# Deformable convolution in a four-layer kernel: GpSimd issues the second chunk's loads, hats go in three lots, and constant products run in a wait

## What is computed

```python
x = x + _L3_conv_ref(_gn(x), L3_conv_weight, L3_conv_bias, L3_conv_off_w, L3_conv_off_b, L3_conv_mask_w, L3_conv_mask_b)

offset = conv2d(x, off_w, off_b)                 # dy, dx for each of 9 taps, image and pixel
mask = jax.nn.sigmoid(conv2d(x, mask_w, mask_b))
samp = deform_sample(x, offset, mask)            # bilinear samples of x at moved places, times mask
out = jnp.einsum('bckhw,ock->bohw', samp, weight.reshape(O, C, K * K))
return out + bias[None, :, None, None]
```

## Time and profile before

| | us |
|---|---|
| median of 3 runs | 539.01 (535.24 to 540.68) |
| the profiled execution | 540.11 |
| its span | 538.3 |

### The profile page before, as it was taken

One profiled execution on the slowest core, in us unless ns is written; L12 is line 12 of the kernel. 1 busy time (PEld: TensorE's weight loads), 2 busy tenths in 40 slices (PEclk: granted clock), 3 DMA queues, 4 the chain that ended last, 5 costly groups with the idle time before them and its releaser, 6 DMA issues. The chain is left out here.

```text
span 538.3 us, 9045 instructions
## 1 busy us (share of the span) xinstructions
PE 421.3 (78%) x3242; PEld 211.8 (39%) x3242; DVE 342.4 (64%) x668; ACT 295.2 (55%) x515; POOL 132.9 (25%) x162
## 2 busy tenths in 40 slices
PE   1415672399999863858999999965977999999995
PEld 1213551245554432512333333333533545455442
DVE  4437787403334537897999999434365878788784
ACT  1359993105145413705888888852675668486441
POOL 4420002200000000665442211104063618155000
PEclk9855997579999956865999999995999999999999
DMA  5500000530000000493220000006464290743302
GB/s 139 160 0 1 0 0 0 119 76 0 1 1 0 1 0 0 127 311 113 82 80 2 4 2 2 2 1 148 99 188 101 58 208 2 185 80 64 70 2 78
DMA packets 20765, 33.77 MB, mean 63 GB/s; under 512 B 5656, under 2 KB 15496, under 8 KB 19956
## 3 DMA queue, kind: packets, MB, share of 16 engines
q1 hardware_dynamic: 16724, 23.70, 18.2%
q0 software_dynamic: 2176, 6.35, 4.3%
q10 hardware_dynamic: 1824, 3.19, 2.2%
HBM read 16.21 MB, written 4.64 MB: 39 GB/s over the span
## 5 line engine op out<-in xcount | busy, mean ns | idle before, releaser
L1308 DVE TENSOR_TENSOR L_s<-L_row_ps,L_cols 128x1024 f32<-128x1024 f32 x72 | 87.7, 1219 | 7.1 <-PE L_row_ps L1473 6.5
L884 DVE TENSOR_REDUCE L_mx<-L_ring 128x2 f32<-128x512 f32 x128 | 83.3, 687 | 10.9 <-PE L_ring L1007 10.3
L939 ACT ACTIVATE L_e<-L_ring 128x512 f32<-128x512 f32 x128 | 73.8, 598 | 20.8 <-PE L_ring L1020 18.8
L1496 PE MATMUL L_acc<-L_s,L_t_sb 128*64 128x256 f32 x576 | 78.0, 392 | 1.4 <-DVE L_s L1308 1.2
L1377 ACT ACTIVATE L_cols<-L_col_ps 128x512 f32<-128x512 f32 x72 | 42.9, 597 | 47.4 <-PE L_col_ps L1483 47.0
L1007 PE MATMUL L_ring<-stacks_k_st,stacks_q_st 64*128 64x256 bf16 x256 | 50.8, 301 | 6.3 <-DVE L_v_all L873 4.6
L1496 PEld LDWEIGHTS L_acc<-L_s,L_t_sb 128*64 128x64 f32 x576 | 34.9, 136 | 34.3 <-DVE L_s L1308 20.7
L1020 PE MATMUL L_ring<-stacks_q_st,stacks_k_st 64*128 64x256 bf16 x256 | 47.1, 281 | 1.3 <-DMA stacks_q_st<-L_m_parts 1.3
L1473 PE MATMUL L_row_ps<-L_hats,L_sel 48*128 48x512 bf16 x144 | 43.2, 381 | 0.0
L1040 PE MATMUL L_ctx_ps<-L_e,L_v_x 128*32 128x256 f32 x512 | 41.1, 395 | 0.0
L370 PE MATMUL L_y<-L_t,all_w_post 128*128 128x256 f32 x96 | 25.1, 416 | 14.3 <-DVE L_t L330 14.3
(11 more groups left out here) (267 smaller groups left out, 788.0 us busy)
## 6 DMA issues: line engine op xcount, KB each, us to landing
L_hats<-L_parts SPq DMA_DIRECT2D x28, 216.0 KB, 4.9
L_hat<-L_offsets SPq DMA_DIRECT2D x20, 192.0 KB, 4.7
L_mask<-L_offsets SPq DMA_DIRECT2D x10, 192.0 KB, 5.1
stacks_q_st<-L_q_parts SPq DMA_DIRECT2D x12, 128.0 KB, 3.9
stacks_k_st<-L_k_parts ACTq DMA_DIRECT2D x12, 128.0 KB, 4.8
stacks_q_st<-L_q_parts POOLq DMA_DIRECT2D x12, 128.0 KB, 2.7
stacks_k_st<-L_k_parts POOLq DMA_DIRECT2D x12, 128.0 KB, 2.9
L_stack<-L_xpad SPq DMA_DIRECT2D x7, 162.0 KB, 5.9
```

Of the source, the lines that this page charges most:

```text
L884: dve.tensor_reduce(mx[:, n % 2, :, head], ring[:, place(step) % 3].rearrange("p (q s) -> p q s", q=2), AX.X, ALU.max).then_inc(max_read, 1)
L939: act.activation(e[:, k], ring[:, 3 + v % 3], ACT.Exp, scale=HD2 ** -0.5).then_inc(e_ready, 1)
L1308: dve.tensor_tensor(s[:, q], row_ps[:, q], cols[:, t % 3:t % 3 + 1].broadcast_to([P, 2, 2 * N]), ALU.mult).then_inc(s_ready, 1)
L1496: mm = pe.matmul(acc[C * e:C * e + C, b, 0:N], t_sb[:, b, h, (KK * e + t) * C:(KK * e + t + 1) * C], s[:, q, h, e * N:(e + 1) * N], start= ...
```

## The change

- **Constant products.** A new function `keep_clock` multiplies the constant `avg2` by itself into a part of `row_ps` that nobody reads: five times after the GroupNorm, then two, two and four times behind the first three `weigh` products.
- **Weigh products.** Three instead of four stand ahead of the first convolution; the fourth comes behind it, and the fifth between `spread_positions(1)` and `spread_masks(1)`.
- **VectorE and ScalarE at the start.** VectorE's copies of the first three products come between the `xpad` steps; ScalarE loads the sigmoid table behind `take_t` of the third product rather than ahead of all.
- **Hats of pair 0 in three lots** of one third each, the second with a semaphore of its own (`second_third_in`, awaited at v = 3).
- **Loads of chunk 1** are issued by GpSimd, between its stores of quad 1 and those of quads 2 and 3. Positions and masks now share one semaphore; for chunk 1 the first third has one (awaited at 48), the second and the last third share another (awaited at 96).
- **`hat_steps`**: the distance and the hat of the last third come ahead of `take_first` of the first third.

The core of the diff:

```diff
+def keep_clock(pe, avg2, out, count):
+    for _ in range(count):
+        pe.matmul(out[:, 0:P], avg2[:], avg2[:], start=True, stop=True)
...
-        hat_in, mask_in = m.sems("hat_in0 hat_in1 hat_in2"), m.sems("mask_in0 mask_in1 mask_in2")
+        hat_in, second_chunk_in, second_third_in = m.sems("hat_in0 hat_in1 hat_in2"), m.sems("second_chunk_in0 second_chunk_in1"), m.sem("second_third_in")
+        def chunk_in(c, j):
+            if c == 1:
+                return (second_chunk_in[0], 48) if j == 0 else (second_chunk_in[1], 96)
+            return hat_in[j], 48 * (c - 1) + (48 if j == 2 and c else 96 if j == 2 else 0)
...
                 sp.wait_ge(off_stored, 128)
-                load_positions(sp, 0, 2)
-                load_masks(sp, 0, 2)
+                load_chunk(sp, 0, 2)
+                sp.wait_ge(parts_ready, 1)
+                send_hats(0, slice(0, THIRD))
                 sp.wait_ge(parts_ready, 2)
-                send_hats(0, slice(0, 2 * THIRD))
-                sp.wait_ge(later_stored, 128)
-                sp.wait_ge(hat_in[2], 32)
-                sp.wait_ge(mask_in[2], 16)
-                for j in range(3):
-                    load_positions(sp, 1, j)
-                    load_masks(sp, 1, j)
+                send_hats(0, slice(THIRD, 2 * THIRD), second_third_in)
                 sp.wait_ge(parts_ready, 3)
...
                 store_masks(pool, slice(1, 2), later_stored)
+                pool.wait_ge(later_stored, 128)
+                for j in range(3):
+                    load_chunk(pool, 1, j)
                 pool.wait_ge(off_ready, 2 * NQ)
-                pool.wait_ge(later_stored, 128)
                 store_offsets(pool, slice(2, NQ), later_stored)
...
+                    if p in (3, 5, 7):
+                        take_first_image(0, p // 2 - 1, p // 2 - 1)
...
-                hat_steps = ((take_distance, 0), (make_hat, 0), (take_distance, 1), (make_hat, 1), (take_first, 0), (take_distance, 2),
-                             (make_hat, 2), (take_first, 1), (take_second, 0), (take_first, 2), (take_second, 1), (take_second, 2))
-                for k in range(4):
+                hat_steps = ((take_distance, 0), (make_hat, 0), (take_distance, 1), (make_hat, 1), (take_distance, 2), (make_hat, 2),
+                             (take_first, 0), (take_first, 1), (take_second, 0), (take_first, 2), (take_second, 1), (take_second, 2))
+                for k in range(3):
                     take_t(0, k, k)
+                act.preload_act_table_set("sigmoid_and_others")
                 take_offsets(0)
+                take_t(0, 3, 3)
...
+                keep_clock(pe, avg2, row_ps[:, 1, 1], 5)
...
+                    if v == 3:
+                        pe.wait_ge(second_third_in, 64)
...
-                for k in range(4):
+                for k in range(3):
                     weigh(0, k, k, k)
+                    keep_clock(pe, avg2, row_ps[:, 1, 1], 2 if k < 2 else 4)
                 conv_offsets(0)
-                weigh(0, 4, 4, 4)
+                weigh(0, 3, 3, 3)
...
                 spread_positions(1)
+                weigh(0, 4, 4, 4)
```

More of the change, by code:

```diff
@@ L1208, in send_hats @@
                             first = C * k + 2 * b + e
-                            sp.dma_start(hats[C * k:C * k + 3 * H, b, e, taps], parts[first:C * k + C:CH, :, taps]).then_inc(hats_in[b], 16)
+                            sp.dma_start(hats[C * k:C * k + 3 * H, b, e, taps], parts[first:C * k + C:CH, :, taps]).then_inc(landed or hats_in[b], 16)
                 def next_chunk(c):
@@ L1361, in take_first @@
                     if c:
+                        act.wait_ge(second_third_in, 64)
                         act.wait_ge(hats_in[0], 64 * c + 64)
```

27 lines of the change are left out of this document (12 added, 15 removed).

## The result

| | before | changed |
|---|---|---|
| median of the runs timed together | 539.16 us (4 runs) | 555.64 us (4 runs: 553.17 to 564.42) |
| ratio, 95% interval | | **1.033** (1.028 to 1.038) |
| profiled execution, time and span | 540.11, 538.3 us | 553.17, 551.3 us |
| mean granted clock, profiled execution | | 0.881 |

The change makes the kernel 3% slower; I had predicted no change, 541.5 us.

The account below looks back on a forecast made before the run. Layer 3 was taken to alternate between an engine-bound loop and waits for hats. First boundary + 1.2, further periods + 3.3, start - 2.0 gave + 2.5 us: 542.6 profiled, 541.5 as median, range 535.5 to 546.5.

Parts of the forecast that it names:

- The start: Before and in the first convolution: constants restore the clock, convolution starts 0.7 us earlier and runs 1.3 shorter; gain 2.0 us.
- the constants do not bring the clock back in time: Rival at the first convolution: it starts at 376.3, as slow as before; total 545.7 us; chance 0.07.
- Part 4: First chunk: GpSimd's loads run beside SP's hats; the second distance waits for both later lots, slot 6 ending at 415.5.
- the landing L: First chunk: time when the second and third lots of chunk 1's loads are in; taken as 408, bounds 404.0 and 410.
- the rival on the clock: Rival in the first chunk: TensorE's clock falls in the new stall, about + 3 us, total 544.5; chance 0.25.
- Part 5: Every chunk: moving `take_first` to slot 6 brings hats 1.65 us later through GpSimd's gapless chain, counted three times.
- two further periods: Later chunks, after the first boundary: the hats' delay counted twice more, 2 x 1.65 = + 3.3 us.
- `take_first` no longer blocks the columns in the first chunk: First chunk: `take_cols` no longer comes late behind `take_first`, so the second stall goes, 1.2 us.
- Part 3: First chunk: hats in three lots make the first `s` 0.7 us earlier and remove the 2.54 us wait.

Follow-up runs that it names:

- a8: Changed kernel with a semaphore for each third of chunk 1's loads and 16 constant products ahead of TensorE's hats wait at later boundaries; 545.05 us, ratio 1.014.
- a3: Changed kernel, GpSimd still issuing chunk 1's loads, but with a semaphore for each third; 544.50 us, ratio 1.012.
- a1: Changed kernel with the old order of ScalarE's steps restored for later chunks; 539.34 us, ratio 1.001.
- c1: Changed kernel with the old order of ScalarE's steps and a semaphore for each third of chunk 1's loads; 538.24 us, ratio 0.994.
- d2: d1 with the new order of ScalarE's steps; 533.25 us, ratio 0.993.
- d3: The same kernel as d2, measured a second time; 531.74 us, ratio 0.986.
- b1: Kernel before with only the new order of ScalarE's steps for later chunks; 545.26 us, ratio 1.020.
- a6: Changed kernel without the new order and without the loads on GpSimd, leaving the start and three hat lots; 537.40 us, ratio 0.996.
- b2: Kernel before with the start alone: constant products, three weights' products ahead of the convolution, copies moved; 536.71 us, ratio 0.996.
- d1: c1 with the first pair's hats sent in thirds in every chunk; 533.99 us, ratio 0.995.
- e1: a3 with the old order of ScalarE's steps for the third and fourth chunk, the new for the second; 542.71 us, ratio 1.007.
- a2: Changed kernel with chunk 1's loads back on SyncE, one semaphore for each third; 548.53 us, ratio 1.009.

## Why the prediction was wrong

**The start** was right in the profiled execution. First `s` 3.2 us earlier against 2.7 forecast; no wait at the first spread, none at the third third's hats. A constant product, priced at 0.63 us at half clock and 0.31 at full, took 0.50 (five in 2.48) and 0.24 (16 in a8's 3.84). The clock's return is less sure than I had it: the half-clock stretch of the GroupNorm ends at 365.5 in the changed kernel's first trace and at 371.5 in its second, with the same products, and in the second the first `s` is only 1.7 us earlier than in before. The first convolution then starts at an offset of 8.2 or of 9.8 to 10.0, so part of the rival "the constants do not bring the clock back in time" is true in many executions: of the 15 traces with constants at the start 10 have the late one.

**Part 4, the landing L, failed.** I had seen the right mechanism: the count at 96 couples slot 2 to the last lot. I took L = 408 with bounds of 404 and 410; less the 2.0 of the start that is an offset of 41.4. The last mask landed at 45.5 in the changed kernel's first trace and at 46.3 in its second, 4.1 and 4.9 us later, and beyond the bound. The loads were issued at about the offset that the forecast gives (29.8 against 29.4), so it is the transfer that was mis-sized. The sum of bytes took the 264 GB/s of the earlier trace rows. The window of the changed kernel while the loads run (columns as in rows 3):

```profile
395.00:405.00 10.00, 5.62 (x38) 2.19 (x34) 3.23 (x5) 2.86 (x5) 6.16 (x9) 0.94 1.02 209
```

The DMA engines are as full (1.02) and move 209 GB/s. At that rate the 2.95 MB need 14.1 us instead of 11.2. The DMA issues of the changed kernel, 388 to 412 (KB each, median us to landing):

```profile
L_mask<-L_offsets POOLq DMA_DIRECT2D x3, 192.0 KB, 7.9
L_hats<-L_parts SPq DMA_DIRECT2D x4, 72.0 KB, 5.5
L_offsets<-L_off POOLq DMA_DIRECT2D x4, 36.0 KB, 10.6
```

The median mask load takes 7.9 us where before, in the same stretch, had 5.5; the last one, which sets L, takes 11.8 where the earlier trace rows had 6.4. SyncE's hats of 72 KB take 5.5 instead of 3.6, and GpSimd's stores of 36 KB 10.6 instead of 3.4. That is the interleaving of which the Trainium skill (DMA: Bandwidth & Descriptors, Issuing engines are not separate DMA queues) speaks, and the trace agrees: the transfers of both issuers became slower together. But its price is not only in the sum of bytes; what made the rate fall to 209 GB/s is open. And the rival on the clock came with it: TensorE's idle 5.74 us at 407.54 ended at half clock. The first chunk cost 9.1 us behind the first `s`, against 1.9 forecast. Against a3 the shared count explains 7.3 of it, and 1.7 is left for the order and the rest; but these parts do not simply add. With the old order the shared count costs 3.7 (a1 against c1), and single traces of the same code differ: d2 and d3, one kernel, take 34.4 and 37.8 us from the first `s` to the boundary. Falls of the clock are part of that. Every trace but before's has one or two in this chunk, b1's too, at 395.6, where its code is still that of before.

**Part 5 was right for its mechanism, and mis-sized by the clock.** The hats are 1.5 us later at a boundary, 1.65 forecast, through GpSimd's gapless chain. What failed is the reading of the earlier trace rows: I took a wait of 2.54 us at 408.72, which the clock survived, as sign that waits of this length are harmless, and priced the fall once, in the first chunk, with a chance of 0.25. At the boundaries it came after waits no longer than that one. In the profiled execution the terms, as the variants give them, sum up: -3.2 for the start, +7.4 for the shared count, 3 x 1.5 for the order and 3 x 2.8 for the clock are +17.1, against +17.2 measured. That this closes so well is partly luck, since the 7.4 could as well have been 5.5. The last of the three falls also made the last stretch longer (34.7 against 32.0 us from chunk 3's boundary to the last sampling), which the forecast of "two further periods" had left out. The rule that I had cited (the Trainium skill, TensorE: Matmul & The Clock Gate, Why this matters for your kernels) warns against idle gaps between bursts of products; I set it against one row and let the row win. The gaps at the boundaries are shorter than those that it names, and the clock fell at 14 of 18 of them all the same. One row of a wait without a fall shows that the clock can survive it, not that it does.

**The rest.** That `take_first` no longer blocks the columns in the first chunk was right in its mechanism (the waits of 2.17 us in before and of 3.41 to 4.08 in a6, b2, c1 and d1 at that split are absent with the new order), and e1 shows that nothing of it was left at the end. Part 3, the three lots, gained its waits but nothing measurable at the end.

## What to carry to other kernels

Price each new or longer wait of TensorE twice: once as its length, once as the products behind it at half clock, and the second at every repetition of the wait. A semaphore that counts two lots makes the first as late as the second; if one has to be shared, share it between things that are wanted together. Before moving work off one queue or changing an order, ask which *last* piece of a transfer the reader waits for: here sending by the piece that is wanted first took away the wait, turned the order's cost into a small gain, and needed no constant products at the boundaries.

## What the runs showed of the hardware

- The clock fell at 14 of 18 waits of 2.3 to 2.65 us at the boundaries, and at none of the 18 of 0.9 to 1.2 us. So waits of equal length end differently: in a2 the wait of 2.47 us at 432.91 left it at 1.00, that of 2.48 us at 467.73 brought it down.
- A fall costs in lumps, 1.4 or 2.8 us of a period (clock low for about 3.5 or 7 us).
- With constant products in the wait the clock stayed full at nine of nine boundaries, but 16 of them, 128x128 f32, take 3.84 us: more than the wait that they were to fill.
- Under gapless products the clock came back after 4.6 us in one execution of the changed kernel (360.9 to 365.5) and after 9.1 in the other (362.4 to 371.5).
